# NF4 weights of a two-layer transformer stack: scaled inside the lookup's PSUM bank, the LoRA product added there, and the rounding rest taken by VectorE instead of GpSimd

## What is computed

```python
x = x + norm(x) @ (weight * block_mask).T                 # masked linear
x = x + norm(x) @ (int4 weights * scale).T + bias         # int4 linear
x = x + nf4_block(norm(x))                                # NF4 + LoRA attention-like sum and gated MLP
x = x + nvfp4_mlp(norm(x))                                # FP4 fake-quantised gated MLP

# the NF4 block; every weight is  W = NF4[codes] * scales(64-wide blocks),  and every product is
#   lin(x, W, A, B) = x @ W.T + (x @ A.T) @ B.T  =  x @ (W + B A).T
attn = (q + k + v) / 3;  o = lin(attn, ...);  x1 = x + o
d = lin(silu(lin(x1, gate)) * lin(x1, up), down);  out = x1 + d        # hidden width 1792, LoRA rank 16
```

## Time and profile before

| | |
|---|---|
| runs | 868.82, 871.15, 869.42 us; median 869.42 |
| profiled execution | 871.42 us, of which 870.1 us are its span (first to last instruction) |
| mean granted TensorE clock | 0.92 |
| busy | PE 737.2 us (85%), DVE 605.0 (70%), ACT 432.7 (50%), POOL 264.0 (30%) |
| NF4 tiles | first lookup at 35 us, last LoRA product at 499 us |

### The profile page before, as it was taken

One profiled execution on the slowest core, in us unless ns is written; L12 is line 12 of the kernel. 1 busy time (PEld: TensorE's weight loads), 2 busy tenths in 40 slices (PEclk: granted clock), 3 DMA queues, 4 the chain that ended last, 5 costly groups with the idle time before them and its releaser, 6 DMA issues.

```text
span 870.1 us, 11393 instructions
## 1 busy us (share of the span) xinstructions
PE 737.2 (85%) x4112; PEld 545.4 (63%) x4112; DVE 605.0 (70%) x1107; ACT 432.7 (50%) x549; POOL 264.0 (30%) x226
## 2 busy tenths in 40 slices
PE   1797664889999989989999888777699799968998
PEld 1564421656777666656666666555478688966886
DVE  4898987563687878889999686765644332557873
ACT  3756665645876867686767112142233111224552
POOL 0223012104474666556666454021111000000000
PEclk9999855989999999999999899787599899997999
DMA  7645678666365666575663110022101110200000
GB/s 279 199 135 170 211 227 266 207 212 215 127 224 183 197 222 218 180 242 188 208 194 119 53 38 25 26 61 61 48 25 39 31 43 27 66 17 12 25 25 37
DMA packets 56039, 110.55 MB, mean 127 GB/s; under 512 B 9888, under 2 KB 20800, under 8 KB 55984
## 3 DMA queue, kind: packets, MB, share of 16 engines
q1 hardware_dynamic: 42560, 78.43, 27.9%
q10 hardware_dynamic: 9040, 17.30, 5.7%
q0 software_dynamic: 4384, 14.09, 5.4%
HBM read 91.65 MB, written 18.15 MB: 126 GB/s over the span
## 4 chain that ended last, share of the span: by engine, by line
PE 51%; DVE 29%; DMA 7%; issue 7%; ACT 3%; SPq 1%; POOL 1%; DVEq 0%; ACTq 0%
PE bank L1098 14%; PE bank L1099 13%; PE bank L1100 13%; DVE hot L1736 4%; PE bank L1202 3%; PE bank L1383 2%; DVE wsum L1754 2%; DMA rep<-codes 2%; DVE x L1854 2%; DVE hot L1739 1%; DVE q_d L1832 1%; DVE q_a L1804 1%; DVE q_r L1798 1%; DVE zt_l L1694 1%; DMA codes<-c 1%
## 5 line engine op out<-in xcount | busy, mean ns | idle before, releaser
L1490 ACT ACTIVATE hot<-rep,levels 128x2048 f16<-128x2048 f16 x96 | 193.5, 2053 | 19.8 <-ACT c L1453 11.9
L1098 PE MATMUL bank<-zt_h,w_h 128*128 128x512 f32 (+1 forms) x232 | 95.9, 413 | 11.4 <-DVE x L1854 8.7
L1202 PE MATMUL bank<-hot,diag 128*32 128x512 f16 x1160 | 80.6, 408 | 17.7 <-DVE wsum L1754 9.4
L2029 POOL TENSOR_TENSOR w_l<-wsum,w_h 128x512 fp32r<-128x512 f32 x46 | 64.3, 1398 | 96.5 <-ACT w_h L1498 89.7
L1099 PE MATMUL bank<-zt_l,w_h 128*128 128x512 f32 (+1 forms) x232 | 92.7, 400 | 0.0
L1100 PE MATMUL bank<-zt_h,w_l 128*128 128x512 f32 (+1 forms) x232 | 92.7, 400 | 0.0
L1098 PE MATMUL bank<-w_h,xq_h 128*128 128x512 f32 (+1 forms) x192 | 74.6, 388 | 4.7 <-DVE w_l L1872 4.7
L1099 PE MATMUL bank<-w_l,xq_h 128*128 128x512 f32 (+1 forms) x192 | 72.6, 378 | 0.0
L1100 PE MATMUL bank<-w_h,xq_l 128*128 128x512 f32 (+1 forms) x192 | 72.6, 378 | 0.0
L1736 DVE TENSOR_SCALAR hot<-rep,levels 128x2048 f16<-128x2048 f16 x58 | 64.0, 1104 | 2.5 <-DMA rep<-codes 1.9
L1202 PEld LDWEIGHTS bank<-hot,diag 128*32 128x32 f16 x1160 | 26.4, 100 | 61.2 <-issue 23.1
(11 more groups left out here) (218 smaller groups left out, 1742.3 us busy)
## 6 DMA issues: line engine op xcount, KB each, us to landing
rep<-codes SPq DMA_DIRECT2D x58, 512.0 KB, 4.6
codes<-c SPq DMA_DIRECT2D x29, 256.0 KB, 4.0
raw<-in_codes_gu_t ACTq DMA_DIRECT2D x14, 512.0 KB, 5.5
sc<-in_scales_gu_t SPq DMA_DIRECT2D x56, 128.0 KB, 3.8
raw<-in_codes_attn_t ACTq DMA_DIRECT2D x8, 512.0 KB, 4.2
raw<-in_codes_down_t ACTq DMA_DIRECT2D x7, 512.0 KB, 5.2
sc<-in_scales_down_t SPq DMA_DIRECT2D x28, 128.0 KB, 2.9
wide_buf<-in_gate_flat SPq DMA_DIRECT2D x5, 512.0 KB, 4.3
```

Source lines behind the costliest of these rows:

```text
L1098: PE.matmul(psum, lh, rh, start=first, stop=False, **kw)
L1202: mm = PE.matmul(bank[32 * q:32 * q + 32, :], lhs, hots[plan.slot[hot_ring(t), (t, m)]][:, q, :], start=m == LOOK_ORDER[0] and part == 0, ...
L1490: S.activation(hots[plan.slot[hot_ring(t), (t, m)]][:], codes_in_place(t), ACT.Relu, bias=bias, scale=slope).then_inc(sem("ramp_act"), 1)
L2029: G.tensor_tensor(wl[:, k, :], wsum[t % 2][:], wh[:, k, :], ALU.subtract).then_inc(sem("made_pool"), 1)
```

## The change

For every `last` tile the weight is finished in the PSUM bank in which it was looked up.

- The lookup uses three banks in turn (5, 6, 7); bank 7 no longer belongs to the LoRA product.
- DVE scales in place: output and input of the scaling are the same bank. In v jobs the scaled product goes to `q_d` and the sum `wsum + q_d` is written to the bank.
- `lora` now stands behind `assemble` in the list. Its matmul waits for DVE's scaled (or merged) of the same tile and accumulates into the same bank (`start=False`). DVE's addition of bank 7 is gone.
- `settle` is split in two. `high_part`: ACT copies the bank to `w_h`, after PE's `made`. `low_part`, one NF4 step later: DVE forms `w_l = bank - w_h`. POOL's L2029 is gone.
- `look(t)` waits for `low_part(t - 3)` (or for scaled, if that tile was not a last one) instead of scaled(t - 2). The products wait for DVE's `made` instead of POOL's.

```diff
     def settle():
+        while halved:
+            p.add("low_part", halved.pop(0))
         while unsettled:
-            p.add("settle", unsettled.pop(0))
+            p.add("high_part", unsettled[0])
+            halved.append(unsettled.pop(0))
...
             if t < tiles:
                 look(t)
-            if t:
-                lora(t - 1)
             if t + 1 < tiles:
                 hits(t + 1)
             if t:
                 assemble(t - 1)
+                lora(t - 1)
                 scales(t + 2)
...
-        if any(t // CU <= i for t in unsettled):
+        while any(t // CU <= i for t in unsettled + halved):
             settle()
...
+    def look_bank(t):
+        return banks[5 + t % 3]
...
             elif kind == "look":
-                bank = banks[5 + t % 2]
-                if t >= 2:
-                    pe.wait_ge(*done("dve", "scaled", t - 2))
+                bank = look_bank(t)
+                if t >= 3:
+                    pe.wait_ge(*done("dve", "made" if jobs[(t - 3) // 2]["last"] else "scaled", t - 3))
...
-                if plan.nth["made", t] > 1:
-                    pe.wait_ge(sem("made_dve"), plan.nth["made", t] - 1)
-                last = PE.matmul(banks[7][:], left[0:stacked, tok(u)], right[0:stacked, :], start=True,
-                                 stop=not plain(j))
+                pe.wait_ge(*done("dve", "scaled" if j["fresh"] else "merged", t))
+                last = PE.matmul(look_bank(t)[:], left[0:stacked, tok(u)], right[0:stacked, :], start=False,
+                                 stop=not plain(j), skip_group_check=True)
...
-                pe.wait_ge(*done("pool", "made", 2 * last_of["gu", g] + 1))
+                pe.wait_ge(*done("dve", "made", 2 * last_of["gu", g] + 1))
...
-            elif kind == "settle":
+            elif kind == "high_part":
-                act.wait_ge(*done("dve", "made", t))
+                act.wait_ge(*done("pe", "made", t))
...
-                S.copy(weight_of(j)[0][:, j["k0"] + t % 2, :], wsum[t % 2][:]).then_inc(sem("made_act"), 1)
+                S.copy(weight_of(j)[0][:, j["k0"] + t % 2, :], look_bank(t)[:]).then_inc(sem("made_act"), 1)
...
             elif kind == "assemble":
...
-                if j["last"]:
-                    dve.wait_ge(*done("pe", "made", t))
-                    dve.wait_ge(*dve_done)
-                    V.tensor_tensor(wsum[u][:], wsum[u][:], banks[7][:], ALU.add).then_inc(sem("made_dve"), 1)
+            elif kind == "low_part":
+                t, = key
+                j = jobs[t // 2]
+                wh, wl = weight_of(j)
+                k = j["k0"] + t % 2
+                dve.wait_ge(*done("act", "made", t))
+                V.tensor_tensor(wl[:, k, :], look_bank(t)[:], wh[:, k, :], ALU.subtract).then_inc(sem("made_dve"), 1)
...
-            elif kind == "settle":
-                pool.wait_ge(*done("act", "made", t))
-                G.tensor_tensor(wl[:, k, :], wsum[t % 2][:], wh[:, k, :], ALU.subtract).then_inc(sem("made_pool"), 1)
```

More of the change, by code:

```diff
@@ L268, in make_plan @@
     p.jobs, p.n_attn, p.last_of = jobs, n_attn, last_of
-    through, made, unsettled = {None}, [0], []
+    through, made, unsettled, halved = {None}, [0], [], []
     p.turns = 0
@@ L343, in assemble @@
             p.note("merged", t)
-            p.take("q_out", 2, ("z", t), ("dve", "merged", t))
+            if not j["last"]:
+                p.take("q_out", 2, ("z", t), ("dve", "merged", t))
         if j["last"]:
@@ L1267, in pe_program @@
                 bank, (vh, vl), (wh, wl) = main(("merge", i)), wring[2], w_out
-                pe.wait_ge(*done("pool", "made", CU * n_attn - 1))
+                pe.wait_ge(*done("dve", "made", CU * n_attn - 1))
                 for m in vacant("main", ("merge", i)):
@@ L1306, in pe_program @@
                 pe.wait_ge(*done("pool", "gu_mul", g, half, 1))
-                pe.wait_ge(*done("pool", "made", 2 * last_of["down", g] + 1))
+                pe.wait_ge(*done("dve", "made", 2 * last_of["down", g] + 1))
                 for m in vacant("main", ("dn", *key)):
@@ L1744, in dve_program @@
                 j, u = jobs[t // 2], t % 2
-                bank, s, sc = banks[5 + t % 2][:], wsum[u][:], scales[t % 3][:]
-                if plain(j):
-                    bank, s = (v.rearrange("p (b c) -> p b c", c=64) for v in (bank, s))
-                    sc = sc[:, 0:8].unsqueeze(2).broadcast_to([P, 8, 64])
+                stays = look_bank(t)[:]
                 dve.wait_ge(*done("pe", "spent", t, LOOK_ORDER[-1]))
                 dve.wait_ge(*landed(("sc", t)))
-                if j["fresh"]:
+                if j["last"]:
+                    into = stays
+                elif j["fresh"]:
+                    into = wsum[u][:]
@@ L1752, in dve_program @@
                     if t >= 2 and jobs[t // 2 - 1]["last"]:
-                        dve.wait_ge(*done("pool", "made", t - 2))
-                    V.scalar_tensor_tensor(s, bank, 1.0 / NF4_SHIFT, sc, ALU.mult, ALU.mult).then_inc(
-                        sem("scaled_dve"), 1)
-                    dve_done = done("dve", "scaled", t)
+                        dve.wait_ge(*done("dve", "merged", t - 2))
                 else:
-                    z = q_out[plan.slot["q_out", ("z", t)]][:].rearrange("p (b c) -> p b c", c=64)
+                    into = q_out[plan.slot["q_out", ("z", t)]][:]
@@ L1759, in dve_program @@
                     for m in vacant("q_out", ("z", t)):
                         dve.wait_ge(*m)
[L1761 to L1769 removed]
+                bank, sc, to = stays, scales[t % 3][:], into
@@ new lines, in dve_program @@
+                if plain(j):
+                    bank, to = (v.rearrange("p (b c) -> p b c", c=64) for v in (bank, to))
+                    sc = sc[:, 0:8].unsqueeze(2).broadcast_to([P, 8, 64])
+                V.scalar_tensor_tensor(to, bank, 1.0 / NF4_SHIFT, sc, ALU.mult, ALU.mult).then_inc(
+                    sem("scaled_dve"), 1)
+                if not j["fresh"]:
+                    dve.wait_ge(*done("dve", "scaled", t))
+                    V.tensor_tensor(stays if j["last"] else wsum[u][:], wsum[u][:], into, ALU.add).then_inc(
+                        sem("merged_dve"), 1)
+            elif kind == "low_part":
[5 more added lines that the diff above has]
+                V.tensor_tensor(wl[:, k, :], look_bank(t)[:], wh[:, k, :], ALU.subtract).then_inc(sem("made_dve"), 1)
```

12 lines of the change are left out of this document (2 added, 10 removed).

## The result

The changed kernel takes **878.86 us** (median of 7 runs, 875.28 to 883.86) against 871.15 for the kernel before in the same series: ratio **1.0092**, 95% interval 1.0055 to 1.0128. It is 7.7 us slower; I had forecast 3.2 us slower. The profiled execution has a span of 877.5 us, 7.4 more than before. One sentence of the part on the change was loose: in the v tiles, too, the scaled product stays in the bank (the second operand of the merge), and only the k tiles' goes to `q_d`.

What follows compares the result with a forecast made beforehand. Between 155 and 500 us PE and DVE were taken to wait for each other in turn. Terms 3.0 + 1.0 + 0.5 - 1.3 = +3.2 us on the 869.4 us median gave 872.6 us; range 863 to 879.5 us.

Steps and rivals of the forecast that it cites:

- Point 3: Lookup with three banks: its wait for the subtraction of three tiles ago is covered by the later scaling wait; 0.
- Point 6: First 178 us: tile 10's LoRA product, now behind scaling and merge, delays its turn; 0 to 1.9 us, taken as +1.0.
- my likeliest case: PE's stalls outweigh DVE's relief: +3.2 us, 872.6 us, own range 869 to 876; chance 0.45.
- Point 8: Before the last down products: PE no longer waits for POOL's L2029 behind `at_l` and starts earlier; -1.3 us.
- DVE is not relieved: Rival: POOL's other work fills L2029's gaps and `hot` stays at 1.1 us; +9.2, 878.6 us, chance 0.15.
- Point 1: DVE's work: 50 additions go, 50 subtractions come, each priced at 0.688 us; sum 0.
- Point 2: DVE scaling in place in the bank: -2.2 to +2.2 us of work, taken as 0, +-0.7 for the range.
- Point 4: LoRA product waits for DVE's scaling: PE stalls 28.9 us, 19.9 come back, both engines 9.0 us late at 507 us.
- Point 5: Without L2029 on POOL, DVE's two-SBUF-input instructions such as `hot` run faster; lateness falls to +1.5 to +4.4, taken as +3.0 us.
- Point 7: Forced subtractions before the second group's first gate/up product, +0.5 us, and at the q, k, v merge, 0.

Runs made afterwards that it cites:

- the old load: Unread POOL subtraction of the old size from tile 12 on: added to the changed kernel 883.28 us, to it reordered as scaling, planes, subtraction 863.35 us.
- two other orders: Changed kernel with LoRA products of tiles 4, 5, 10, 11 at the next step's head, 875.25 us; changed kernel with subtraction behind scaling in the same step, 871.52 us.

## Where the prediction was right and where it was off

The direction held: slower, since PE waits for DVE at the LoRA product and the relief of DVE does not pay for it. Points 3 and 6 failed, and the total of 878.86 lies outside my likeliest case (869 to 876). That it lies inside the whole range (863 to 879.5) is partly luck: the first two stretches lost 15.0 us where points 3 to 7 had 4.5, and the third won 6.5 where point 8 had 1.3. It is the number of the rival "DVE is not relieved" (878.6), whose mechanism is refuted: `hot` fell to 908 ns.

- *Point 1, no change in DVE's work.* Right: 682 ns for 688.
- *Point 2, scaling in place.* 691 ns against 680, 0.5 us over 50. Right.
- *Point 3, the lookup's wait is worth 0.* **This step failed.** PE waited 22.6 us there, and moving the subtraction alone gave 7.3 us back. "1.5 us of DVE against 1.3 us of PE" took the lookup at its fast duration. Behind the two longest of these waits after tile 16 (tile 20, 2.50 us, and tile 48, 3.87 us) it took 2.32 and 2.33 us, longer than DVE's 1.5, and there the shadow is gone; behind the shorter ones (tiles 21, 34, 47 and 53, 0.59 to 1.75 us) it took 1.26, as assumed. That is under 2 us. The idle time was mostly shadowed, as argued (15 of 21.4 us moved on). What the step left out altogether is the slower matmuls: with the subtraction moved, PE is busy 4.1 us less between tiles 4 and 16 and 6.2 us less between 16 and 57 for the same work, and 1.8 us more behind it.
- *Point 4, stalls before the LoRA product.* The stalls came, but the 42 tiles stalled for 15.8 us, not 28.9, and at other tiles than named: most at tile 42 (3.00 us), 17 (2.54) and 32 (1.84), and tiles 33, 47 and 51 for less than 0.1. At tile 33 PE had waited already, before the lookup of tile 34, for the subtraction:

```profile
314.77 1.26 PE L1209 MATMUL bank<-hot,diag 128*32 128x512 f16 x20 [1.75 <-DVE w_l L1781]
```

  With the 11.1 us before the lookups of these tiles the sum is 26.9, near the 28.9 that was carried. What failed is the address, and that a stall was priced by its idle time alone.
- *Point 5, relief.* `hot` 908 ns, within 0.9 to 1.0 us. DVE lost 28.5 us of work, more than the 19 counted: small FP4 instructions shrank too (`q_c` at L1801 1.19 us at 501.70 before, `q_c` 0.24 now). On the path the old load is worth 4.4 to 5.3 us by the medians (4.8 to 6.3 by the ratios), near the 6 that I took. Right in size, with the reservation on POOL's own queue.
- *Point 6, first 178 us, +1.0.* **The second that failed**: +7.9 from tile 4 to 16. Tile 10's turn started at 120.95 us, forecast 119.6, and its LoRA product at 119.54, forecast 118.1; DVE had come 1.3 us later to its scaling than in the kernel before. The mechanism was right there, but tile 4 has the same two matmuls behind the same merge and was not looked at, and the clock was held to be what it was.
- *Point 7.* Not to be seen: PE waits 1.1 us for `w_l` at a gate/up product, and the merge of q, k and v 3.7 us for `wo_l`, 5.4 before.
- *Point 8, -1.3.* Right for its gap (4.11 us, now 2.76), but the stretch gained 6.5. A second gap, before the down products at 506.41, was missed: `x += bank` stood on DVE behind FP4 instructions that ran beside `at_l` and L2029 on POOL and took up to five times as long. For the two that stretched most (`q_c` 1.19 us for 0.24, `q_r` 0.80 for 0.18) that is 1.6 of the 3.80 us of this gap; the rest is not accounted for. From the timeline of the kernel before:

```profile
501.70 1.19 DVE L1801 TENSOR_SCALAR q_c<-q_r,gm 128x32 f32<-128x32 f32 x1
...
506.41 0.50 PE L1098 MATMUL bank<-w_h,at_h 128*128 128x512 f32 x1 [3.80 <-DVE x L1854]
```

The last gap, where the subtraction no longer follows `at_l` on POOL:

```profile
549.57 1.26 POOL L2065 TENSOR_TENSOR at_l<-ztok,at_h 128x512 fp32r<-128x512 f32 x1 [4.52 <-ACT at_h L1529]
```

```profile
550.80 0.48 PE L1106 MATMUL bank<-w_h,at_h 128*128 128x512 f32 x1 [2.76 <-issue]
```

## What to carry to other kernels

When a change hands a wait to an in-order engine, ask first what stands ahead of the awaited instruction there: the same instructions in another order were worth 21 us here, and the part of that order that the kernel without the change can take was worth nothing there. Put what the bottleneck engine waits for at the front of a step, and what nobody waits for until the next one behind it, but not at the head of the next. Price a stall of TensorE by its idle time and by the slower matmuls that may follow it, and look at every place with the same pattern, not at the first one found.

## What the runs showed of the hardware

- A stall of PE can cost more than itself. After 12 us at a granted clock of 1.00 (2.4 GHz) PE stood idle for 3.87 us, and the lookup behind it ran at 0.50 (1.2 GHz), 2.33 us for 1.26. Between tiles 4 and 16 the same matmuls took 56.35 us at a mean granted clock of 0.74 as changed, and 51.90 or 52.28 us at 0.81 in two other orders whose idle time there was no shorter.
- DVE's subtraction with one input in a bank took 673 to 692 ns, whether POOL worked beside it (26 of 50) or not. With both inputs in SBUF (the kernel before with its rest on DVE) it took 673 to 684 ns alone and 678 to 2839 beside POOL (31 of 50). The Trainium skill has the rule ("GPSIMD Engine Reference", Specifications: contention where VectorE has two SBUF inputs, or a two-port mode); by it the change's subtraction had to be free of POOL, and the trace agrees.
